# Node update of a graph network: the add of beta to x on GpSimd, cut in two parts and released by VectorE's progress

## What is computed

```python
out = agg.reshape(n, HID) + (x @ Wskip + bskip)
h = jax.nn.gelu(out, approximate=False)
y = x + h                                  # x: the first layer's normalised input
mu = jnp.mean(y, axis=-1, keepdims=True)
var = jnp.var(y, axis=-1, keepdims=True)
return (y - mu) / jnp.sqrt(var + 1e-05) * gamma + beta
...
x = x + _L0_gnn_ref(_layernorm(x, axis=-1), edge_index, ...)   # call this x2
x = x + _L0_ffn_ref(_layernorm(x, axis=-1)[None], ...)[0]      # starts with a norm of x2
```

## Time and profile before

| | us |
|---|---|
| median of 3 runs | 4070.35 (4068.75 to 4072.07) |
| the profiled execution, first to last instruction | 5874.6 |
| node update in it (from 3543 to 3734) | 191 |
| routing walk and experts in it (from 3734 to 5735) | 2001 |

### The profile page before, as it was taken

The page is one execution under the profiler, slowest core; times in us unless marked ns, Lnnn a source line. Parts: engine busy times, 40 slices in busy tenths (PEclk is TensorE's granted clock), DMA queues, the critical chain, the costliest instruction groups (busy, mean ns, idle before and its releaser), DMA issues. The chain is left out here.

```text
span 5874.6 us, 106076 instructions
## 1 busy us (share of the span) xinstructions
PE 3912.2 (67%) x26108; PEld 2753.9 (47%) x26109; DVE 3464.7 (59%) x9273; ACT 2543.2 (43%) x6305; POOL 2589.4 (44%) x2723
## 2 busy tenths in 40 slices
PE   7857777777777777777777773355666666666550
PEld 3335555555555556555555563233434343443330
DVE  8856666666666666666666668434444444444348
ACT  4445555555555555554555555223333333333320
POOL 3244444444444444444445441444444444445540
PEclk9978888888888888888888885577877787777765
DMA  6455555555555555555556555111111111111117
GB/s 212 147 163 165 155 168 163 163 161 168 156 159 163 161 168 156 165 158 165 154 166 172 159 150 177 44 15 18 21 19 21 19 21 19 22 18 19 20 21 263
DMA packets 367690, 683.50 MB, mean 116 GB/s; under 512 B 70294, under 2 KB 240482, under 8 KB 367074
## 3 DMA queue, kind: packets, MB, share of 16 engines
q0 software_dynamic: 157888, 427.05, 27.9%
q1 hardware_dynamic: 183106, 223.68, 11.5%
q10 hardware_dynamic: 26080, 25.70, 1.5%
HBM read 588.41 MB, written 87.78 MB: 115 GB/s over the span
## 5 line engine op out<-in xcount | busy, mean ns | idle before, releaser
L746 POOL DMA_INDIRECT KV<-kv_d,src_i x1564 | 1482.7, 948 | 1677.7 <-DVE msg L839 1232.4
L1389 POOL DMA_INDIRECT re_src<-src_tab_d,rsrc x1024 | 974.5, 952 | 978.7 <-SPq L1399 675.7
L1013 PE MATMUL agg_ps<-msg,oh 128*128 128x264 f32 x3512 | 1085.8, 455 | 229.7 <-issue 218.4
L1013 PEld LDWEIGHTS agg_ps<-msg,oh 128*128 128x128 f32 x3512 | 744.4, 222 | 414.2 <-issue 282.7
L1597 PE MATMUL ex_y_ps<-ex_w,ex_hid 128*112 128x256 f32 x1792 | 586.6, 461 | 301.6 <-issue 299.1
L966 PE MATMUL Q<-q,ohT 128*128 128x256 bf16 x5328 | 753.0, 297 | 15.6 <-issue 13.9
L839 DVE TENSOR_TENSOR msg<-KV,weigh_ps 128x1056 f32<-128x1056 f32 x439 | 545.7, 1243 | 268.6 <-ACT weigh_ps L920 250.1
L1516 ACT COPY re_ohT<-re_ohT_ps 128x1024 bf16<-128x1024 bf16 x179 | 181.0, 1011 | 1075.0 <-remote 1010.6
L966 PEld LDWEIGHTS Q<-q,ohT 128*128 128x128 bf16 x5328 | 531.4, 105 | 117.4 <-issue 19.5
L909 ACT ACTIVATE square<-iota_b,off 128x128 bf16<-128x128 bf16 x1784 | 569.2, 392 | 0.3
L1597 PEld LDWEIGHTS ex_y_ps<-ex_w,ex_hid 128*112 128x112 f32 x1792 | 363.7, 214 | 434.1 <-issue 366.0
(11 more groups left out here) (264 smaller groups left out, 6199.0 us busy)
## 6 DMA issues: line engine op xcount, KB each, us to landing
q<-q_d SPq DMA_DIRECT2D x446, 192.0 KB
y_d<-ex_y ACTq DMA_DIRECT2D x56, 448.0 KB
rg_ye<-y_d SPq DMA_DIRECT2D x7, 3584.0 KB, 11.8
KV<-kv_d,src_i POOLq DMA_INDIRECT x1564
nu_xs<-xs_d SPq DMA_DIRECT2D x7, 2688.0 KB, 11.9
re_src<-src_tab_d,rsrc POOLq DMA_INDIRECT x1024
kv_d<-pr_kv SPq DMA_DIRECT2D x49, 260.0 KB, 2.2
xs_d<-pr_xs SPq DMA_DIRECT2D x49, 256.0 KB, 2.4
```

Of the source, the lines that this page charges most:

```text
L746: pool.indirect_dma_start(out=KV[:, t % (KVR * G), :], out_offset=None, in_=k.kv_d, in_offset=bass.IndirectOffsetOnAxis(ap=k.src_i[:, t:t ...
L1013: m = pe.matmul(agg_ps[:, 0:HEADS * HW], oh32[ring(s, 2)][:, t, :], msg[ring(s, 2)][:, t, :, :].rearrange("p h e -> p (h e)"), start=False ...
L1389: pool.indirect_dma_start(out=gs[:, t % (RING * RG), :], out_offset=None, in_=k.src_tab_d, in_offset=bass.IndirectOffsetOnAxis(ap=k.rsrc[: ...
```

## The change

The add over a whole block (128 x 1792) becomes two adds: the last three tiles (128 x 768), then the first four (128 x 1024). The first waits, beside the load, until L1201 of the block before is done (for block 0: until L1181 of block 0 is done); the second waits until L1192 of the same block is done. Each raises `xb` by one, and VectorE's wait ahead of L1201 counts two a block. `parts` stands for ((0, 4), (4, 7)).

```diff
@@ in VectorE's turn
-                    v.wait_ge(xb, i + 1)
+                    v.wait_ge(xb, i * 2 + 2)
                     ch.on(v.tensor_tensor(x2[s][:, :, :], x2[s][:, :, :], xs[s][:, :, 2 * D:3 * D], ALU.add))
@@ in GpSimd's block
                 for i in range(NB):
                     x = xs[i % 2][:, :, 2 * D:3 * D]
                     pool.wait_ge(landed[i % 2], (i // 2 + 1) * 16)
-                    pool.tensor_tensor(x, x, bc(bet[:, :].unsqueeze(1), [P, CW, D]), ALU.add).then_inc(xb, 1)
+                    for n, (a, b) in enumerate(parts[::-1]):
+                        if n:
+                            pool.wait_ge(back, i * KB + 1)
+                        elif i:
+                            pool.wait_ge(back, (i - 1) * KB + X2)
+                        else:
+                            pool.wait_ge(s_in, 1)
+                        pool.tensor_tensor(x[:, a:b, :], x[:, a:b, :], bc(bet[:, :].unsqueeze(1), [P, b - a, D]), ALU.add).then_inc(xb, 1)
```

## The result

The changed kernel takes 4049.5 us (median of five, 4048.0 to 4052.7) against 4070.4 before (4068.8 to 4072.1); the ratio is 0.995, with a 95% interval of 0.9939 to 0.9961. That is 20.9 us less, where 19.4 was forecast, and the time is in the range of the prediction (4046 to 4060).

A forecast was written before the change was run, and what follows sets the result against it. VectorE's serial chain was taken to bound the node update; removing 18.85 us of L1176 stalls and 0.59 of L1192, with nothing added by the parts or waits, gave 4070.35 - 19.4 = 4050.95, about 4051 us, range 4046 to 4060.

The forecast's parts named there:

- 5 x 3.77 and 0.59: VectorE's node-update chain: stalls removed from L1176 in blocks 2 to 6 and L1192 in block 0, together 19.4 us.
- The parts' length: GpSimd's two adds: estimated at 1.85 us for the first part and 2.38 for the second.
- The upper bound of 3.96: GpSimd's parts: if cutting gained nothing, each part would take 3.96 us.
- the 0.35 worked out: L1163: at the parts' upper bound it stands for 0.35 us, at most 14 times, 4.9 us.
- The room: From L1154 to L1163, 3.71 us of one-input instructions: parts fit with 1.2 us or more spare, cost nothing.
- What is late next: Node update with turns cut from 23.43 to 19.7 us: VectorE still waits for nobody, so all 19.4 us are saved.
- The load's spare: Block 2's load before L1181: landing 11.75 us after issue, reader at 12.50, spare 0.75, the least of all covers.
- Taking the saving unscaled: Timed median: the profiled saving taken whole, 4070.35 - 19.4 = 4050.95, about 4051 us.
- the saving of 13.4 us by the ratio of the times: Node update in timed runs: if shorter by the whole program's ratio, 0.693, the saving is 13.4 us, time 4057.
- rival 2: Stall isn't removed: timed loads land elsewhere, or late GpSimd stands in L1176's way again; 4070 us, chance 0.09.
- Rival 4: Routing walk: TensorE's mean clock falls below 0.748 and takes the gain back; at 0.74, 4083 us; chance 0.03.
- The prediction's sign for it: Routing walk in the profile after: it lasts 2001 us with a clock of 0.76.

The follow-up runs named there:

- the run with the late second part: Changed kernel with the add's second part released by L1163 of the first normalisation instead of L1192: 4060.9 us, ratio 0.9972.
- the version with filled gaps: Changed kernel with VectorE work (L1171, L1173, copies L1185, L1186) put into its wait before L1161, and xb counted once a block: 4044.8 us, ratio 0.9939.
- the whole late add: Against the kernel before, one uncut add a block, released by L1163 of the first normalisation: 4069.4 us, ratio 0.9990.

## Why the prediction was right, and where it was not

**The stall.** 5 x 3.77 and 0.59, 19.4 us, is what the chain lost (19.41). That the whole of it would go, and that it needed the add to be moved rather than cut, the two runs with one half of the change each show: the place alone gives 18.4 of the 19.4 and the cut alone nothing. The opening says that the engines meet only at semaphores; this stall is a meeting without one.

**The parts' length.** 1.85 and 2.38 were estimated from two rows and 1.81 and 2.35 measured. The upper bound of 3.96 was far off; but the whole add in the same place showed what it would have cost: it ended 0.37 us into L1163, close to the 0.35 worked out, and cost 0.23 us a block, since the price is a little less than the overlap. GpSimd began 0.05 to 0.11 us after the release, for the 0.1 taken.

**The room.** Here the reasoning was incomplete. The prediction took "one input in SBUF" as the mark of what GpSimd doesn't hold up, and so counted L1163 as the first instruction at risk. The mark holds for L1154, L1158 and L1173. It doesn't for L1171, which stood up to 2.40 us. L1171 comes right behind L1163, so the free stretch was the same, and no number of the sum changed. The Trainium skill, SBUF — State Buffer, Who interferes with whom, names `tensor_scalar` among the operations that can take the pair of ports shared with GpSimd; the 2.40 us of the run with the late second part agree with it, and the prediction had not made use of it.

**What is late next.** Most of the slack worked out ahead was found: the gelu of the looped turns starts 1.1 us after L1181's end, at its place without harm; L1181 of block 2 starts 12.51 us after its load's issue, where 12.50 was forecast; TensorE's products are ready for their copies. The turn of block 4 is 19.75 us against 19.7. The load's spare was not as sure as 0.75 us. That figure takes one landing, 11.75 us after the issue, as fixed, but block 2's load landed after 11.5 and 11.9 us in the two profiles of the changed kernel and after 11.3 to 12.3 in all eleven profiles (12.1 in the second of before, 12.3 with the cut alone). So the spare was 1.0 and 0.6 us in the changed kernel, and with the latest of these landings it would have been 0.2. In the version with filled gaps the skip add was ready 11.78 us after the issue, the load landed at 12.2, and the add began at 12.68; what the 0.5 us behind the landing are, the runs don't show.

**The timed runs.** Taking the saving unscaled was right. The profiled execution's extra time lay ahead of the node update and in the routing walk, not in the node update. So the saving of 13.4 us by the ratio of the times wasn't the case, and rival 2 (another landing in ordinary runs) fell with the second profile of before: one landing was another, the price the same.

**What was left out.** The chain lost 19.4 us, but from the first transfer's issue to GpSimd's first instruction of the next stage the kernels went from 189.9 and 190.5 us to 172.3 and 172.4, 17.6 to 18.2. Most of the rest is in the tail: the last 28 products of TensorE took 4.33 and 5.12 us in the two profiles of before, with a mean granted clock of 0.73 and 0.62 over them, a mixture of 1.2 and 2.4 GHz, and 6.17 in both of after, with 0.50, which is 1.2 GHz throughout. The second profile of before, and then the first of after:

```profile
2608.67:2613.80 5.13, 5.12 (x28) 5.00 (x28) 0.00 (x0) 0.00 (x0) 0.00 (x0) 0.62 0.00 0
...
2587.51:2593.70 6.19, 6.17 (x28) 6.04 (x28) 0.00 (x0) 0.00 (x0) 0.00 (x0) 0.50 0.00 0
```

The whole add after L1192 had 4.20 and the kernel without adds 5.08, and the cut without release, as slow as before, 6.17; so this is worth 1 to 2 us either way and doesn't go with the saving. The prediction hadn't priced it. Rival 4, the clock of the routing walk, didn't occur: 0.91 and 1363 us in both kernels' ordinary profiles. The prediction's sign for it, 2001 us at 0.76 again, failed, because it took the long execution for the usual one; nothing in the sum hung on it. Between those profiles the whole span differs by 20.5 us, 18.0 of it in this stage; 1.6 more lie ahead of it (it starts at 2427.2 and 2425.6) and 0.9 behind it, in stages the change doesn't touch. Why those differ, and the 1.5 us between the first median difference (20.9) and the forecast, these runs don't settle. The chain was forecast to within 0.1 us; that the medians came so near as well (20.9 and 19.0 for 19.4) is in part luck, since the stage itself gave only 17.6 to 18.2 and the runs of one kernel spread over 2 to 11 us.

## What to carry to other kernels

When an instruction stands still for the length of another engine's, look at what the two need in common before looking at semaphores: here no wait on any list showed 19 us of stall, only one product of 4193 ns among 418s did. A helper engine's work that nobody waits for still has to be given a time to begin, and a semaphore that the busy engine raises anyway, just ahead of instructions that don't collide, gives it at no cost. Price the place first and the size second: in the wrong place a cut add cost as much as a whole one, in the right place an uncut one cost a microsecond and a half.

## What the runs showed of the hardware

- A GpSimd add over SBUF of 128 x 768, 1024 and 1792 numbers (f32) took 1.81, 2.35 and 3.97 us: 0.19 us and 2.11 ns a number, by the first two and within 0.01 us for the third.
- It kept out two-input instructions of VectorE (L1163 0.40 us for 0.17, a product of L1176 4.19 for 0.42, L1181 5.64 for 2.02, L1192 2.61 for 2.02, L1198 4.18 for 2.02) and the one-input L1171, a tensor_scalar of f32 (0.21 us alone, up to 2.40), and didn't touch bn_stats (L1154, 2.39 us for seven both ways), bn_aggr (L1158, 0.58 for seven) or a reciprocal (L1173, 0.50).
- Where the add was running first, the VectorE row that met it lost 0.13 to 0.16 us less than the time from its start to the add's end, in the 27 such cases of four variants and the second profile of before: 0.23 of 0.37 (L1163 under the whole add), 2.19 of 2.34 (L1171), 3.30 of 3.45 (the first group of L1176 under the whole late add), 3.62 of 3.76 (L1181 in the second profile of before). The other way round it is the same: the first two adds of the earlier trace rows began 1.99 and 0.90 us before L1181 and L1192 ended, and took 5.80 and 4.71 us, 0.15 less than this and the add's 3.96 together.
- Which instruction pays is decided within a tenth of a microsecond: L1171 starting 0.01 us after the add paid 2.2 us, and starting 0.08 or 0.09 us before it nothing.
- A wait for a value that is worked out in a register (i * 2 + 2) cost VectorE 0.08 us each in the four looped turns, where nothing else held it; the wait for i + 1 cost nothing.
